# Layer 3's router in a one-core GNN and mixture-of-experts kernel: eight contractions of 8 columns, or four groups of 32 array columns side by side

## The reference, cut to what matters

```python
C = 256; HID = 1024; E = 8
H = jax.nn.gelu(xf @ W1 + b1, approximate=False)            # 625 x 1024
probs = jax.nn.softmax((H @ Wg + bg) / TEMP, axis=-1)       # the router: 1024 -> 8
assign = jnp.argmax(probs, axis=-1)
for e in range(Wd.shape[0]):
    y = H @ Wd[e] + bd[e]                                   # 1024 -> 256 for each expert
    out = out + jnp.where((assign == e)[:, None], probs[:, e:e + 1] * y, 0.0)
```

## Time and profile before

| what | value |
|---|---|
| time, median of 3 runs | 972.86 us (970.52 to 976.18) |
| the profiled execution: its own time | 975.67 us |
| its span, first to last record | 973.5 us |
| mean granted TensorE clock in it | 0.949 of full speed |
| TensorE busy, matmuls | 892.7 us, 92% of the span |
| VectorE busy | 447.8 us, 46% |
| ScalarE busy | 281.1 us, 29% |
| GpSimd busy | 182.1 us, 19% |

### The profile page before, as it was taken

How to read it: one execution, slowest core, us unless ns; L and a number is a source line. 1 busy time by engine, 2 the same in 40 slices (tenths; PEclk the granted TensorE clock), 3 DMA queues, 4 the chain that set the end, 5 groups by cost and what they waited for, 6 DMA issues and landing times.

```text
span 973.5 us, 15475 instructions
## 1 busy us (share of the span) xinstructions
PE 892.7 (92%) x5638; PEld 710.7 (73%) x5638; DVE 447.8 (46%) x1433; ACT 281.1 (29%) x625; POOL 182.1 (19%) x177
## 2 busy tenths in 40 slices
PE   6999998999999999999996778999999999899897
PEld 4776656889999877889875667777887554665665
DVE  7988555522222421632278976423434142340623
ACT  5111263122222114233347853332111111114210
POOL 2201000122221200045427751000101100000231
PEclk9999899999999999899988979999998899799899
DMA  8303001288885603159241000353100000320696
GB/s 296 142 2 92 1 1 38 96 303 315 320 325 192 235 1 130 54 187 322 98 164 68 1 1 1 130 192 120 45 1 14 19 1 1 130 96 35 206 344 230
DMA packets 28007, 120.42 MB, mean 124 GB/s; under 512 B 5401, under 2 KB 10032, under 8 KB 20132
## 3 DMA queue, kind: packets, MB, share of 16 engines
q1 hardware_dynamic: 22362, 104.39, 30.1%
q0 software_dynamic: 5280, 14.95, 4.6%
q10 hardware_dynamic: 295, 0.14, 0.1%
HBM read 106.11 MB, written 13.36 MB: 123 GB/s over the span
## 4 chain that ended last, share of the span: by engine, by line
PE 71%; DVE 15%; DMA 5%; issue 5%; ACT 2%; DVEq 1%; POOL 1%; SPq 0%; POOLq 0%; ACTq 0%
PE PS L817 8%; PE PS L473 6%; PE PS L441 5%; PE PS L832 5%; PE PS L884 4%; PE PS L868 4%; PE PS L485 4%; PE PS L552 4%; PE PS L627 2%; PE PS L908 2%; PE PS L959 2%; PE PS L948 2%; PE PS L1268 2%; DMA HT<-flat_rows,route 2%; DVE ring L1991 2%
## 5 line engine op out<-in xcount | busy, mean ns | idle before, releaser
L441 PE MATMUL PS<-const 128*128 128x128 f32 x674 | 92.8, 299 | 5.8 <-DVE X L1358 2.1
L441 PEld LDWEIGHTS PS<-const 128*128 128x128 f32 x674 | 88.2, 212 | 10.2 <-DVE X L1358 2.9
L817 PE MATMUL PS<-HT,ring 128*128 128x128 f32 x680 | 79.1, 275 | 3.3 <-DVE HT L1512 1.7
L817 PEld LDWEIGHTS PS<-HT,ring 128*128 128x128 f32 x680 | 78.4, 192 | 4.6 <-issue 3.9
L2655 POOL TENSOR_TENSOR col<-col,power 125x4 f32<-125x4 f32 (+2 forms) x13 | 11.9, 917 | 315.4 <-DVE col L1351 226.5
L2715 POOL DMA_INDIRECT slot_rows<-ST,route x41 | 41.4, 1010 | 151.1 <-ACT ST L2429 96.0
L2753 POOL TENSOR_TENSOR arena<-arena,ring 125x625 f32<-125x625 f32 x40 | 55.7, 1416 | 34.3 <-ACT arena L2517 30.1
L1911 DVE TENSOR_TENSOR HT<-HT,PS 128x256 f32<-128x256 f32 (+1 forms) x51 | 19.1, 376 | 89.8 <-ACT HT L2418 71.6
L627 PE MATMUL PS<-HT 125*128 125x126 bf16 x530 | 41.7, 230 | 6.8 <-DVE HT L1722 6.7
L1049 PE MATMUL PS<-w,HT 125*64 125x125 f32 x400 | 30.3, 305 | 18.0 <-DVE w L2010 18.0
L832 PE MATMUL PS<-ring,HT 128*128 128x256 f32 x204 | 46.8, 380 | 0.0
(11 more groups left out here) (472 smaller groups left out, 1712.3 us busy)
## 6 DMA issues: line engine op xcount, KB each, us to landing
ring<-in_experts SPq DMA_DIRECT2D x17, 1386.0 KB
ring<-in_experts SPq DMA_DIRECT2D x17, 768.0 KB, 6.0
ring<-in_experts SPq DMA_DIRECT2D x11, 1026.0 KB
arena<-in_experts SPq DMA_DIRECT2D x10, 1024.0 KB
ring<-in_experts SPq DMA_DIRECT2D x7, 1024.0 KB, 7.6
arena<-in_experts SPq DMA_DIRECT2D x6, 1026.0 KB
arena<-in_gnn SPq DMA_DIRECT2D x5, 1024.0 KB, 5.9
ring<-in_experts SPq DMA_DIRECT2D x8, 513.0 KB, 3.7
```

The lines of the kernel that those rows point to most:

```text
L441: pe.matmul(PS[:, bank, 0:128], ident, ident, start=True, stop=True)
L817: mm = pe.matmul(PS[:, bank, at:at + SLOTS], both[:, j, k, m * 128:(m + 1) * 128], xs[0][i % 2][:, k, :], start=(k == 0), stop=(k == KD - 1))
```

## The change

The eight contractions of the router are dealt out over four groups of 32 array columns: contraction k writes PSUM partitions 32(k mod 4) to 32(k mod 4)+31, so that each group adds two of the eight. For this the weights' 8 columns are padded with zeros to 32 in a new view `wide_router` (128 x 8 x 32). The four partial sums lie 32 partitions apart, and zero in between. ScalarE copies all 128 partitions with the bias column (zero beyond its first 8 rows) into `group_logits` (128x625). The five transposes become five products: stationary a 128x125 piece of `group_logits`, moving a 128x8 matrix `group_sum` that has the 8x8 identity at each of the four groups, so that the turning also adds the groups. `combT` becomes the first 8 rows of `group_logits`. Both new operands lie in `rows`, and GpSimd fills them once, between the last addition of layer 2's attention and the next `rstd`: a memset of 128x256, a copy of 128x64, and four copies of 32x8, each behind a wait for the one before.

```diff
+GROUP = 32
-        combT = sb("combT", [NX, N])
+        group_logits = sb("group_logits", [128, N])
+        combT = group_logits[0:NX, :]
+        wide_router = rows[:, 0:M3 * GROUP].rearrange("p (k n) -> p k n", k=M3)
+        group_sum = rows[:, M3 * GROUP:M3 * GROUP + NX]
-            def logits_turned(src_t, w, kk):
+            def grouped_logits(src_t):
+                groups = 128 // GROUP
+                pe.wait_ge(pattern_ready, 9)
                 pe.wait_ge(act_free, n["a"] - 1)
                 for c0, c in HALVES:
                     bank = act_bank()
                     if c0:
                         pe.wait_ge(act_free, n["a"] - 2)
-                    for k in range(kk):
-                        mm = pe.matmul(PS[0:NX, bank, 0:c], w[:, k, :], src_t[:, k, c0:c0 + c],
-                                       start=(k == 0), stop=(k == kk - 1))
+                    for k in range(M3):
+                        at = k % groups * GROUP
+                        mm = pe.matmul(PS[at:at + GROUP, bank, 0:c], wide_router[:, k, :], src_t[:, k, c0:c0 + c],
+                                       start=(k < groups), stop=(k >= M3 - groups))
                     mm.then_inc(act_full, 1)
                 bank = dve_bank()
                 for t, c0, c in tiles(N):
                     if t in (0, HALF_TILES[1][0]):
                         pe.wait_ge(act_free, n["a"] - (t == 0))
-                    mm = pe.transpose(PS[0:TP, bank, t * NX:(t + 1) * NX], combT[:, c0:c0 + c], ident[0:NX, 0:NX])
+                    mm = pe.matmul(PS[0:TP, bank, t * NX:(t + 1) * NX], group_logits[:, c0:c0 + c], group_sum,
+                                   start=True, stop=True)
                 mm.then_inc(dve_full, 1)
-                logits_turned(hid, wv(wr, WR, "l3", 8), 8)
+                grouped_logits(hid)
-                    act.activation(combT[:, c0:c0 + c], PS[0:NX, b, 0:c], ACT.Identity,
-                                   bias=COLS(cols, name, NX)).then_inc(act_free, 1)
+                    act.activation(group_logits[:, c0:c0 + c], PS[:, b, 0:c], ACT.Identity,
+                                   bias=COLS(cols, name)).then_inc(act_free, 1)
+            pool.memset(wide_router, 0.0).then_inc(wuv_ready, 1)
+            pool.wait_ge(wuv_ready, 6)
+            pool.tensor_copy(wide_router[:, :, 0:NX], wv(wr, WR, "l3", M3)).then_inc(pattern_ready, 1)
+            for j, p in enumerate(range(0, 128, GROUP)):
+                pool.wait_ge(pattern_ready, 5 + j)
+                pool.tensor_copy(group_sum[p:p + GROUP, :], ident[p:p + GROUP, p:p + NX]).then_inc(pattern_ready, 1)
+            pool.wait_ge(pattern_ready, 9)
             rstd()
```

## The result

The changed kernel takes 964.48 us (median of 20 runs, 956.96 to 972.12); the kernel before, run beside it, takes 970.91 us (median of 20, 967.21 to 977.80). The ratio is 0.9924, 95% interval 0.9900 to 0.9949. So the change makes the kernel faster by 0.4 to 0.8%, about 4 to 7 us. A ratio here is the recorded one: it is taken over fast runs alone (a run more than 1.5% above the fastest of its kernel is left out), and it isn't the quotient of the medians, which differs from it by up to 0.3%.

What follows compares the result with a forecast made beforehand. TensorE bound the kernel: the router's thirty-two records, one 8.53 us piece on the chain, release both branches. Products -6.3, table load +0.65, turning +0.2: about -5.5, so 972.86 - 5.5 = 967.4 us; range 964.0 to 971.5.

Steps and rivals of the forecast that it cites:

- the full factor: Router's sixteen products on TensorE: four groups run fully side by side, 5.07 and 3.38 us becoming 1.27 and 0.84.
- Two groups at a time: Rival at the router's products: the array gives only a factor of two; 4.0 us gained, 968.9 us; chance 0.13.
- The estimate from its factor for three groups: Router's products: from the skill's 2.38 for three groups, four would be 3.2 times as fast, 2.6 us instead of 2.1.
- the 0.65 counted as bare: ScalarE before its first logits copy: the table load, formerly hidden under the first eight contractions, now costs 0.65 us.
- 0.2 us longer on the path: Between ScalarE's last copy and VectorE's copy: the turning, now ten records instead of five, costs 0.2 us more.
- Value 0: GpSimd's six new operations, under 2.5 us altogether, fall into its 11.46 us of idle time and cost nothing.
- its term 972.86: Last step of the sum: median of the three runs shown, in us, from which the 5.5 us gain was subtracted.
- the sum of the parts: Router path: products -6.3, table load +0.65, turning +0.2, together about -5.5 us.
- the range of 964.0 to 971.5: Range in us for the changed kernel's median, meant to hold 8 in 10.
- The rival: Expert blocks: half clock catches one block more or less, 2.0 us either way; a fifth of forecast's 0.66, 0.05 beyond.

Runs made afterwards that it cites:

- 9: Changed kernel plus 25 filler products (5.7 us) on TensorE ahead of the router's first contraction; 972.80 us, ratio 1.0001 to the kernel before.
- 2: Changed kernel with two groups of 64 columns instead of four of 32; 968.51 us, ratio 0.9992 to the kernel before.
- Experiment 4: Changed kernel with ScalarE's table load and one-element activation put behind its two copies of the logits; 963.15 us, ratio 0.9923 to the kernel before.
- 7: Changed kernel with four of the router's eight contractions left out in each half, so nodes go to other experts; 961.78 us (4 runs), ratio 0.9893.
- 3: Changed kernel with all eight contractions one after the other in one group of 32 columns; 972.40 us, ratio 1.0034 to the kernel before.
- 5: Kernel before with only GpSimd's six operations added, their results unread; 969.93 us, ratio 0.9981 to the kernel before.
- 1: The changed kernel measured again, no edit; 967.76 us, ratio 0.9958 to the kernel before.
- 4b: The changed kernel with the table load behind the copies of the logits, measured again; 964.66 us, ratio 0.9926 to the kernel before.
- 6: Changed kernel with 2 instead of 10 filler products ahead of the bias product; 966.14 us, ratio 0.9943 to the kernel before.
- 8: Changed kernel with the table load behind the copies and 2 instead of 10 filler products; 965.57 us, ratio 0.9958 to the kernel before.
- 3b: The one-group version of the changed kernel, measured again; 970.67 us, ratio 0.9972 to the kernel before.

## Why the prediction was right, and where it was off

**The path.** The router stood on the path of both branches, and what it lost arrived at the end: 5.60 us in the distance, 5.0 to 6.0 at equal clock, and none of it with the time put back (9). That DMA was idle at that moment and every later transfer is released by a step of the shifted work was the reason given; it was not tried by itself, and nothing measured speaks against it.

**Four groups side by side.** Taken at the full factor, 2.11 us and a tail; it is 2.31 with the tail, with the four loads of a round in 0.13 us. That four would keep what two showed was an inference from the two, and only these runs bear it out. Two groups at a time would have left 4.4 us (2). The rule of the Trainium skill ("TensorE: Matmul & The Clock Gate", "Part 3: Packing small matmuls — row/col tiling") that a load overlaps running matmuls only in other rows isn't what this trace shows: all four groups use all 128 rows, and thirty-two loads of 0.11 us, 3.5 us if they stood alone, fit into 2.31 us beside the stream. The estimate from its factor for three groups, 2.6 us for the products, was too slow as well.

**The copies and the table load.** Forecast: copies at 2.11 us after the first record (893.04 less 890.93), because the table load is late next; measured 2.00. Experiment 4 takes it away and wins 0.40 us of the 0.65 counted as bare: the first copy starts 0.47 us earlier, and the second then waits for its products. In 7 the copies start at 2.00 us as well, so behind the table load shorter products are worth nothing.

**The turning.** 0.2 us longer on the path was forecast; one group (3) shows 0.27. VectorE's copy was forecast 4.00 us after the first record, measured 3.96.

**GpSimd.** Value 0; 1.6 us in an idle stretch of 11.5, and nothing in the times (5).

**The number, where it was off.** The step that failed is the last of the sum, "so the predicted median is 972.86 - 5.5": its term 972.86 was mis-sized. It took the median of three runs as the kernel's own. Twenty runs beside the changed kernel gave 970.91, later 35, 25 and 23 runs 970.8, 970.2 and 971.1, so the term was 1.9 us too high. From 970.9 the same 5.5 us lead to 965.4; measured were 964.48 and 967.76. Counted from the kernel's level of 970.9 the forecast of 967.4 was a gain of only 3.5 us, or 0.36%, where the first comparison has 6.4 us by the medians and 0.76% by the ratio, though the sum of the parts was right to 0.1 us in the profile (5.60 against 5.5). "Medians of three runs of this kernel lie a microsecond or two apart" was no reason to take that term as known: 2 us are more than a third of the gain that was to be forecast. That the range of 964.0 to 971.5 still held 964.48, by 0.5 us, owes more to its width than to its centre. What the first comparison has beyond 5.6 us (0.8 us by the medians) is not explained; the second has 2.5 us less than 5.6, and the two together, at equal clock, 5.6.

**The clock.** The rival priced an expert block more or less at half clock at 2.0 us. In the profile after the first block did run at full clock, 3.67 instead of 5.59 us, but from VectorE's copy to the end only 0.8 us are saved. Part was lost ahead of that block: the filler took 4.10 us at half clock, 2.47 in the kernel before, and the block's transposes start 19.6 us after VectorE's copy instead of 18.4. Part was lost behind it: TensorE waits longer for the later gather. The filler before and the wait for the later gather before and after, then a stretch of the changed kernel:

```profile
912.28 2.47 PE L441 MATMUL PS<-const 128*128 128x128 f32 x20 [0.65 <-DVE route L1644]
953.04 1.09 PE L1243 MATMUL PS<-const,HT 128*128 128x128 f32 x8 [0.40 <-DMA HT<-flat_rows,route]
948.60 1.09 PE L1251 MATMUL PS<-const,HT 128*128 128x128 f32 x8 [1.13 <-DMA HT<-flat_rows,route]
945.00:950.00 5.00, 3.87 (x36) 2.53 (x34) 0.70 (x2) 0.60 (x1) 1.10 (x2) 1.00 1.02 424
```

The DMA engines were busy throughout (share 1.02) while TensorE stood idle for 1.13 of these 5 us, so here work that was ready earlier met transfers that weren't.

One pair of profiles doesn't price the fall, though, and the other profiles on record say more. They are one execution each (7, with its other work, left out). In the six that have four groups and the time freed (changed, 1, 4, 4b, 6, 8) the first block ran at full clock in five, all but 4; in the other six (before, 2, 3, 3b, 5, 9) in none: 4.30 us in 2, 5.48 to 5.75 in the rest. From VectorE's copy to the end it is 70.6, 70.6, 70.7, 70.8 and 72.2 us with that block at full clock, the profile after being the 72.2, and 71.8 to 73.4, in the mean 72.6, with it at 5.48 us or more. The means differ by 1.6 us, so the rival's 2.0 was not far off, and the profile after is the least favourable of its kind. So the change may well move the fall in its favour besides shortening the router. Whether that is worth anything in the median isn't shown: the time put back (9) gives +0.4 ± 1.0, and the changed kernel's 5.6 us at equal clock need no more than the distance. What makes the clock fall at one place in one run and not in the next stays open.

## What to carry to other kernels

Where the stationary side of a contraction has 32 columns or fewer and it sums over many blocks, deal the blocks to four column groups and let a product that is needed anyway add them: the stream, here of float32 products with 375 and 250 columns, is divided by four. Before counting the gain, look at what hid under the long version on the other engines (here a table load of 1.28 us), and move it, since it is what the path waits for next. And don't subtract a small gain from a median of three runs: with single runs up to 17 us apart, take more of them and sort them by their granted clock first. One profile prices a wandering effect such as the clock's fall no better than three runs price a median.

## What the runs showed of the hardware

- Column groups scale without a loss that shows, up to four: 8.59, 4.43 and 2.31 us for the same sixteen float32 products in one, two and four groups, some 0.2 us of it tail, moving operands of 128 partitions each; a round of four records of 375 columns comes every 0.31 us, as a single one did (0.317). Weight loads of 32 columns last 0.11 us, four of them together 0.13 us.
- The stationary width costs nothing in the stream: 8 and 32 columns, 8.59 and 8.61 us.
- Float32 turning by a product (ten records) instead of a transpose (five): 0.27 us more on the path.
- Over 206 runs a us at half clock goes with 0.36 us of time, not the 0.5 that it would cost if all of it were on the path. By that slope the step from 0.948 to 0.962 of mean clock is 10 us; the changed kernel's single runs at these clocks lie 6 to 15 us apart.
- In one execution an idle time of 1.34 us in an otherwise busy stretch was followed by half clock (7), while in one execution of the changed kernel 0.38 us at the same place was not. Two cases don't show that the idle time was the cause.
